# Self-attention values kept at 64 features a head, q and k projected for the second-next batch, and the layer norms' ends moved to the next score stage

## The chip, the cores and the metric

One core of a Trainium2 chip runs the whole kernel in one launch. The metric is the device time of one execution in microseconds (us). The core has four compute engines that the text calls TensorE (PE in the rows; PEld is its weight load), VectorE (DVE), ScalarE (ACT) and GpSimd (POOL), and SyncE (SP), which here only issues the DMAs. Each runs its own list of instructions strictly in order; semaphores join them.

## What is computed

The input x has 16 batches of 256 tokens with 128 features, in float32. Each batch passes through one decoder layer:

```python
x = layernorm(x + attn(x))        # 16 heads of 64, two null keys and values, ALiBi bias, causal
x = layernorm(x + xattn(x, ctx))  # 16 heads of 8 features, 64 context tokens
x = layernorm(x + ffn(x))         # eight groups of two batches; 128 -> 512 -> 128, no activation between
# inside attn, for a normalised xn:
q, k = l2norm(xn @ w_q) * q_scale, l2norm(xn @ w_k) * k_scale
sim = q @ k.T * 8 - slope[h] * distance      # masked above the diagonal
out = concat_heads(softmax(sim) @ (xn @ w_v)) @ w_out
```

## The kernel before, in words

All 16 batches are unrolled; `schedule` (L344) calls each engine's own `iteration(i, w, g)` for i = 0 to 15. A batch has two tiles t of 128 tokens. The order of the work is written out by hand, once for each engine, and the engines meet only through semaphores: whatever stands in an engine's list waits for what stands ahead of it. `stages(i)` (L350) says which parts exist at the ends of the loop. Iteration i does these things:

- **Score stage.** TensorE multiplies q and k of batch i (`scores`, L552) into the PSUM banks S0, S1 and S2. VectorE adds the bias and finds the row minimum of the negated score (`mask_scores`, L998, 32 instructions a batch). ScalarE takes the exponentials with their row sums (`exponentials`, L1315, 32 a batch). VectorE works out the denominators (`denominators`, L1015), and GpSimd multiplies the probabilities by them in 4 chunks for tile 0 and 8 for tile 1 (`norm_probs`, L1513).
- **Value products.** For each of the 12 chunks TensorE transposes four blocks of probabilities into bank T0 or T1 (`turn_probs`, L578), VectorE or ScalarE copies them to SBUF (`copy_pT`), and TensorE weighs the values with them (`weigh_values`, L589). Before the change w_v and w_out are multiplied together at the start (`merged_values`, `split_m`), so a head's values have 128 features and all heads add up in one PSUM tile `psY[t]`; the projection `project_v` (L528) then has 8 chunks of 512 columns. Every projection chunk is three matmuls, since the operands are split into two parts (`split_product`, L439).
- **q and k of batch i + 1**: `xn_turn` and `split_xnT`, 8 chunks of `project_qk` through the banks J0 and J1, of which VectorE copies three and ScalarE five, `square_qk` (ScalarE), `sum_squares` and `norms` (VectorE), `norm_qk` (GpSimd), `turn_qk`, `copy_qT`, `copy_kT`. This whole chain lies inside one iteration.
- **Second attention of batch i - 1** (`cross_scores`, `cross_shift`, `cross_exponentials`, `cross_denominators`, `norm_cross`, `turn_cross_probs`, `weigh_cross_values`, `merge_cross_heads`), its layer norm (ln3) and its feed-forward (`x2_turn`, `feed_forward`, `add_h2`), and half a layer norm more (`ln4_end` comes one iteration later). The layer norm after the first attention (ln2) and the turn of its result (`x1_turn`, `cross_q`) stand at the end of iteration i.

A layer norm is `ln_begin` (statistics, L844), a seed of the inverse root by ScalarE (`ln_seed`, L1249) and `ln_end` (L863): three small VectorE instructions that depend on one another (L857, L859, L861) and two of 128 x 128 (L870). `norms` has the same three small ones. `take` (L433) makes TensorE wait until the last reader of a PSUM bank is done.

## Time and profile before

| what | us |
|---|---|
| median of 3 runs | 1009.04 (1008.38 to 1009.17) |
| the profiled execution | 1014.34 |
| its span, first to last instruction | 1012.2 |

| engine | busy us | share of the span |
|---|---|---|
| TensorE | 849.9 | 84% |
| VectorE | 802.7 | 79% |
| ScalarE | 660.7 | 65% |
| GpSimd | 425.7 | 42% |

The profile is of one execution. An engine's busy time is the time in which at least one of its instructions runs; matmuls overlap, so the length of a single matmul is a latency, and what it costs is the distance from its start to the start of the next. The chain that ended last is 45% TensorE, 25% VectorE and 18% ScalarE.

### The profile page before, as it was taken

How to read it: one execution, taken by the hardware profiler on the slowest of the kernel's cores; microseconds unless marked ns; L12 is line 12 of the kernel's file. 1: busy time of each engine (PE TensorE's matmuls, PEld its weight loads, DVE VectorE, ACT ScalarE, POOL GpSimd, SP SyncE). 2: the span in 40 equal slices, each digit the busy share in tenths (PEclk: the TensorE clock that was granted, in tenths of full speed). 3: DMA queues.
4: the chain of work that ended last, by engine and by line, in shares of the span. 5: the costliest groups of instructions: out<-in, count | busy, mean ns of one | idle time of the engine just before them, and what ended most of it. 6: DMA issues, size and time to landing. Idle time of an engine off the chain costs nothing.

```text
span 1012.2 us, 18717 instructions
## 1 busy us (share of the span) xinstructions
PE 849.9 (84%) x6181; PEld 663.4 (66%) x6181; DVE 802.7 (79%) x2564; ACT 660.7 (65%) x1938; POOL 425.7 (42%) x356
## 2 busy tenths in 40 slices
PE   6898888888888898888889889888888888888774
PEld 5667666765766676576767657666765766676552
DVE  6665779788888978898897888788787988888545
ACT  4475767757685766767676675767667576766532
POOL 0244162543616253361635346173534617253431
PEclk9799999999999999999999999999999999999795
DMA  6000000000100000000100001000100001000000
GB/s 189 6 1 6 6 27 7 6 12 6 28 12 6 6 13 26 6 6 12 27 6 7 11 6 28 11 6 7 27 11 7 6 12 27 1 6 6 6 1 10
DMA packets 26414, 15.56 MB, mean 15 GB/s; under 512 B 4304, under 2 KB 25552, under 8 KB 26320
## 3 DMA queue, kind: packets, MB, share of 16 engines
q1 hardware_dynamic: 26320, 14.38, 5.0%
q8 instruction: 50, 0.82, 0.3%
q14 instruction: 44, 0.36, 0.1%
HBM read 12.27 MB, written 2.10 MB: 14 GB/s over the span
## 4 chain that ended last, share of the span: by engine, by line
PE 45%; DVE 25%; ACT 18%; issue 6%; POOL 4%; DMA 2%; DVEq 0%; ACTq 0%; POOLq 0%
PE psY L600 12%; ACT pr L1319 9%; PE psS L566 6%; PE psT L586 5%; PE psS L636 4%; ACT sq L1291 3%; POOL pr L1519 3%; PE psJ L441 3%; PE psS L548 3%; PE psJ L443 2%; PE psJ L442 2%; DVE xp L1061 2%; DVE xmax L1059 2%; DVE ssq L957 2%; ACT xpT L1367 2%
## 5 line engine op out<-in xcount | busy, mean ns | idle before, releaser
L1519 POOL TENSOR_TENSOR pr<-pr,rden 128x512 f32<-128x512 f32 x192 | 192.9, 1040 | 379.2 <-ACT pr L1319 195.8
L600 PE MATMUL psY<-val,pT 128*128 128x128 f32 x1536 | 206.5, 281 | 31.3 <-ACT pT L1334 23.7
L1319 ACT ACTIVATE pr<-pr,nmin 128x256 f32<-128x256 f32 (+1 forms) x512 | 225.3, 443 | 10.8 <-DVE nmin L1004 10.2
L600 PEld LDWEIGHTS psY<-val,pT 128*128 128x128 f32 x1536 | 186.6, 193 | 41.8 <-issue 22.2
L1004 DVE CUSTOM_DVE_ANT_0 pr<-psS,alibi,nullmin 128x256 f32<-128x256 f32 (+1 forms) x512 | 183.7, 414 | 26.4 <-PE psS L566 24.4
L1510 POOL TENSOR_TENSOR qk<-qk,rn 128x1024 f32<-128x1024 f32 x64 | 121.1, 1913 | 88.8 <-DVE x L870 50.2
L586 PE MATMUL psT<-ident,pr 128*128 128x128 f32 x768 | 116.9, 279 | 20.2 <-POOL pr L1519 20.2
L566 PE MATMUL psS<-kT,qT 64*128 64x256 f32 (+1 forms) x1024 | 111.7, 346 | 19.3 <-DVE nmin L1004 12.9
L586 PEld LDWEIGHTS psT<-ident,pr 128*128 128x128 f32 x768 | 88.9, 143 | 39.9 <-POOL pr L1519 32.7
L566 PEld LDWEIGHTS psS<-kT,qT 64*128 64x128 f32 x1024 | 78.2, 189 | 48.5 <-DVE nmin L1004 19.4
L1319 ACT ACTIVATION_READ_ACCUMULATOR pr<-pr,nmin 128x1 f32 x512 | 96.6, 189 | 0.0
L1304 ACT ACTIVATE val<-psJ 128x512 f32<-128x512 f32 x112 | 66.5, 594 | 25.6 <-PE psJ L443 25.1
L1059 DVE TENSOR_REDUCE xmax<-psS 128x8 f32<-128x512 f32 x64 | 43.9, 686 | 49.1 <-PE psS L636 49.1
L1334 ACT ACTIVATE pT<-psT 128x512 f32<-128x512 f32 x112 | 65.4, 585 | 26.3 <-PE psT L586 26.1
L957 DVE TENSOR_REDUCE ssq<-sq 128x16 f32<-128x1024 f32 x64 | 76.3, 1211 | 7.3 <-ACT sq L1291 5.9
L1283 ACT ACTIVATE qk<-psJ 128x512 f32<-128x512 f32 x80 | 47.5, 594 | 51.5 <-PE psJ L443 50.0
L441 PE MATMUL psJ<-wqk_hi,xnT_hi 128*128 128x512 f32 x128 | 61.9, 484 | 19.8 <-DVE xnT_lo L951 19.2
L1526 POOL TENSOR_TENSOR xp<-xp,xrden 128x1024 f32<-128x1024 f32 x32 | 60.9, 1902 | 29.2 <-DVE xrden L1068 28.5
L1367 ACT ACTIVATE xpT<-psT 128x512 f32<-128x512 f32 x64 | 37.7, 592 | 53.8 <-PE psT L660 53.7
L1028 DVE COPY pT<-psT 128x512 f32<-128x512 f32 x80 | 54.2, 677 | 21.6 <-PE psT L586 21.6
L548 PE MATMUL psS<-ident,qk 128*128 128x128 f32 x512 | 68.6, 278 | 2.3 <-DVE qT L994 2.3
L441 PEld LDWEIGHTS psJ<-wqk_hi,xnT_hi 128*128 128x128 f32 x128 | 24.9, 195 | 65.1 <-issue 31.5
(138 smaller groups left out, 1663.5 us busy)
## 6 DMA issues: line engine op xcount, KB each, us to landing
...
```

What stands on the lines that cost most here:

```text
L441: pe.matmul(dst, hi, whi, start=True, stop=False)
L548: mm = pe.transpose(psS[isk][:, P * j:P * (j + 1)], qk[t][:, col:col + P], ident[:])
L566: mm = pe.matmul(psS[score_bank(t, c)][:, keys * j:keys * (j + 1)], qT[r, h // 2, P * t:P * (t + 1)], kT[r, h // 2, 0:keys], start=True, s ...
L586: mm = pe.transpose(psT[c % 2][:, P * j:P * (j + 1)], pr[t][:, h, P * kt:P * (kt + 1)], ident[:])
L600: mm = pe.matmul(psY[t], pT[c % 4][:, P * j:P * (j + 1)], val[:, kt, P * h:P * (h + 1)], start=(blk == 0), stop=False)
L957: steps.mark(dve.tensor_reduce(ssq[:, t, H * half:H * (half + 1)], sq[:, HD * half:HD * (half + 1)].rearrange("p (h d) -> p h d", d=DH), A ...
L1004: dve.tensor_tensor_reduce(pr[t][:, h, :], psS[score_bank(t, c)][:, keys * j:keys * (j + 1)], alibi[:, h, SEQ - keys:SEQ], 1.0, nullmin[:, ...
L1304: act.activation(val[:, c // 4, 512 * (c % 4):512 * (c % 4) + 512], psJ[c % 2][:], ACT.Copy).then_inc(v_copied_act, 1)
L1319: act.activation(pr[t][:, h, :], pr[t][:, h, :], ACT.Exp, bias=nmin[:, t, h:h + 1], scale=-1.0, accum_out=dparts[:, t, h, 0:1]).then_inc(e ...
L1334: act.activation(pT[c % 4][:], psT[c % 2][:], ACT.Copy).then_inc(pT_copied_act, 1)
L1510: pool.tensor_tensor(v, v, rn[:, t, H * k:H * (k + 1)].unsqueeze(2).broadcast_to([P, H, DH]), ALU.mult).then_inc(qk_normed, 1)
L1519: pool.tensor_tensor(pr[t][:, hs, :], pr[t][:, hs, :], rden[:, t, hs].unsqueeze(2).broadcast_to([P, heads, P * (t + 1)]), ALU.mult).then_i ...
```

## The change

Values: w_v is split and used as it is, w_out stays in SBUF, `project_v` has 4 chunks instead of 8, and the product is turned around: the values (128 keys x 64 features) are the stationary operand, the transposed probabilities move, and the result of an even head lands in partitions 0 to 63, of an odd head in 64 to 127. Eight heads (a group) fill one bank, ScalarE copies it (`copy_aoT`, four a batch), and `join_heads` multiplies it by w_out, four matmuls a group. VectorE's copies of q, k and values all go to ScalarE.

Order: q and k are projected for batch i + 2 (two buffers for `qk`, `xnT`, `val`), the value projection of batch i + 1, the ends of ln3, of the feed-forward and of ln4 of batch i - 2, and `x1_turn` and `cross_q` of batch i - 1 stand in the score stage of iteration i, and `norm_qk` of batch i + 1 stands at GpSimd's head and between its two `norm_probs`. The input load of batch i + 3 takes the place of that of i + 2 at the head of SP's list. Iteration 0 does the q and k chain of batch 1 as well. Several buffers are shared (x1T, xoT and x2T; xpT and pT; x2b and r1), with waits for it. The diff, cut to its core:

```diff
 MASKED = 1e30
 
 QK_CHUNKS = 8
-V_CHUNKS = 8
-
-QK_DVE, QK_ACT = (0, 1, 3), (2, 4, 5, 6, 7)
-V_DVE, V_ACT = (2,), (0, 1, 3, 4, 5, 6, 7)
+V_CHUNKS = 4
+
+QK_DVE, QK_ACT = (), (0, 1, 2, 3, 4, 5, 6, 7)
 PT_DVE, PT_ACT = (0, 2, 6, 8, 10), (1, 3, 4, 5, 7, 9, 11)
...
 
 
...
             def project_v(n, c):
-                t, j = c // 4, c % 4
-                if isinstance(n, int) and n == 0 and c < 4:
-                    pe.wait_ge(m_split, 2 * (c // 2) + 2)
-                if c in V_ACT:
-                    take(f'J{c % 2}', v_copied_act, chunks_to(V_ACT, n, c))
-                else:
-                    take(f'J{c % 2}', v_copied_dve, chunks_to(V_DVE, n, c))
+                t, j = c // 2, c % 2
+                if isinstance(n, int) and n == 0 and c < 2:
+                    pe.wait_ge(wv_split, c + 1)
+                take(f'J{c % 2}', v_copied, V_CHUNKS * n + c + 1)
                 tok, col = slice(P * t, P * (t + 1)), slice(512 * j, 512 * (j + 1))
-                split_product(psJ[c % 2][:], xnT_hi[:, tok], xnT_lo[:, tok],
-                              m_hi[:, col], m_lo[:, col]).then_inc(v_ready, 1)
+                split_product(psJ[c % 2][:], xnT_hi[n % 2][:, tok], xnT_lo[n % 2][:, tok],
+                              wv_hi[:, col], wv_lo[:, col]).then_inc(v_ready, 1)
...
                 heads, keys = (4, P) if t == 0 else (2, SEQ)
-                if t == 0 and pair == 0:
-
-                    pe.wait_ge(kT_copied, 2 * NT * b + 1)
+                half = pair if t == 0 else pair // 2
+                pe.wait_ge(qT_copied, 2 * NT * b + 2 * t + half + 1)
+                pe.wait_ge(kT_copied, 2 * NT * b + 2 * t + half + 1)
...
             def turn_probs(b, c):
                 t, first = (0, 0) if c < TILE_PC[0] else (1, TILE_PC[0])
                 pe.wait_ge(probs_normed, PC * b + c + 1)
-                if c >= 2:
-                    evacuated(b, c - 2)
+                if c in PT_DVE:
+                    take(f'T{c % 2}', pT_copied_dve, chunks_to(PT_DVE, b, c))
+                else:
+                    take(f'T{c % 2}', pT_copied_act, chunks_to(PT_ACT, b, c))
...
+            def group_bank(t, g):
+
+                return ('S2', psS[2]) if t == 1 and g == 0 else ('Y', psY_bank)
+
             def weigh_values(b, c):
+
                 t, first = (0, 0) if c < TILE_PC[0] else (1, TILE_PC[0])
+                group = TILE_PC[t] // 2
+                g, within = divmod(c - first, group)
+                name, bank = group_bank(t, g)
                 if c == 0:
-                    pe.wait_ge(v_copied_dve, len(V_DVE) * (b + 1))
-                    pe.wait_ge(v_copied_act, len(V_ACT) * (b + 1))
-                if c == TILE_PC[0]:
-                    pe.wait_ge(y_added, NT * b + 1)
+                    pe.wait_ge(v_copied, V_CHUNKS * (b + 1))
+                if within == 0:
+                    take(name, aoT_copied, AC * b + 2 * t + g + 1)
                 evacuated(b, c)
-                for j in range(4):
+                blocks = [0, 1, 2, 3] if t == 0 else [0, 2, 1, 3]
+                for j in blocks:
                     blk = 4 * (c - first) + j
                     h, kt = blk // (t + 1), blk % (t + 1)
-                    mm = pe.matmul(psY[t], pT[c % 4][:, P * j:P * (j + 1)], val[:, kt, P * h:P * (h + 1)],
-                                   start=(blk == 0), stop=False)
+                    pair, r = h // 2 - 4 * g, slice(DH * (h % 2), DH * (h % 2) + DH)
+                    mm = pe.matmul(bank[r, P * pair:P * (pair + 1)], val[b % 2][:, kt, DH * h:DH * (h + 1)],
+                                   pT[c % 4][:, P * j:P * (j + 1)], start=(kt == 0), stop=(kt == t))
                 mm.then_inc(pv_done, 1)
+
+            def join_heads(b, t, g):
+
+                pe.wait_ge(aoT_copied, AC * b + 2 * t + g + 1)
+                if g == 0:
+                    take('Y' if t == 0 else 'S2', y_added, NT * b + t + 1)
+                for k in range(4):
+                    pe.matmul(psY[t], aoT[g][:, P * k:P * (k + 1)], wo[:, 4 * g + k, :],
+                              start=(g == 0 and k == 0), stop=False)
 
...
@@ -677,23 +683,23 @@
             def merge_cross_heads(b):
                 pe.wait_ge(xoT_copied, b + 1)
                 for t in range(NT):
-                    mm = pe.matmul(psS[2][:, P * t:P * (t + 1)], xoT[:, P * t:P * (t + 1)], xwo[:],
+                    mm = pe.matmul(psY_bank[:, P * t:P * (t + 1)], xoT[:, P * t:P * (t + 1)], xwo[:],
                                    start=True, stop=True)
                 mm.then_inc(y2_ready, 1)
 
             def x2_turn(b):
...
@@ -923,14 +945,13 @@
                         steps.mark(last)
                 last.then_inc(wn_split, 1)
 
-            def split_m(c):
-                dve.wait_ge(m_ready, c + 1)
-                hi, lo = (m[:].rearrange("p (c r d) -> p c r d", r=2, d=P)[:, 4 * (c // 2):4 * (c // 2) + 4, c % 2, :]
-                          for m in (m_hi, m_lo))
-                ps = psS[c % 2][:].rearrange("p (c d) -> p c d", d=P)
-                steps.mark(dve.tensor_copy(hi, ps))
+            def split_wv(c):
+                dve.wait_ge(vo_loaded, 16 * 2)
+                col = slice(512 * c, 512 * (c + 1))
+                steps.mark(dve.tensor_copy(wv_hi[:, col], wv_raw[:, col]))
                 steps.wait(dve)
-                dve.tensor_tensor(lo, ps, hi.bitcast(F32), ALU.subtract).then_inc(m_split, 1)
...
@@ -975,18 +997,14 @@
                 steps.wait(dve)
                 steps.mark(dve.tensor_tensor(nullneg[:], nullmul[:], nullbias[:], ALU.add))
                 steps.wait(dve)
-                steps.mark(dve.tensor_reduce(nullmin[:], nullneg[:].rearrange("p t (h n) -> p t h n", n=NULLS),
-                                             AX.X, ALU.min))
-                steps.wait(dve)
+                dve.tensor_reduce(nullmin[:], nullneg[:].rearrange("p t (h n) -> p t h n", n=NULLS),
+                                  AX.X, ALU.min).then_inc(nulls_scored, 1)
+                dve.wait_ge(nulls_scored, n + 1)
...
+                act.activation(val[n % 2][:, c // 2, 512 * (c % 2):512 * (c % 2) + 512], psJ[c % 2][:],
+                               ACT.Copy).then_inc(v_copied, 1)
+
+            def copy_aoT(b, t, g):
+                act.wait_ge(pv_done, PC * b + (TILE_PC[0] if t else 0) + (TILE_PC[t] // 2) * (g + 1))
+                bank = psS[2] if t == 1 and g == 0 else psY_bank
+                act.activation(aoT[g][:], bank[:], ACT.Copy).then_inc(aoT_copied, 1)
 
             def copy_kT(n, k):
                 t, half = k // 2, k % 2
...
             def copy_xqT(b):
                 act.wait_ge(xqT_ready, b + 1)
-                act.activation(xqT[:], psJ[1][:, 0:SEQ], ACT.Identity, bias=xb[:, 0:1]).then_inc(xqT_copied, 1)
+                act.activation(xqT[:], psT[1][:, 0:SEQ], ACT.Identity, bias=xb[:, 0:1]).then_inc(xqT_copied, 1)
...
             copy_qk(0, 4)
             copy_qk(0, 5)
```

The order of a full, odd iteration after the change, read off the diff, one list for each engine:

```
PE:
scores(i,0,0); x1_turn(i-1); project_v(i+1,0); scores(i,0,1); cross_q(i-1); project_v(i+1,1); scores(i,1,0);
x2_turn(i-2); project_v(i+1,2); scores(i,1,1); feed_forward(i-2); project_v(i+1,3); turn_probs(i,0); scores(i,1,2);
turn_probs(i,1); turn_nulls(i,0); weigh_values(i,0); turn_probs(i,2); scores(i,1,3); weigh_values(i,1);
turn_probs(i,3); weigh_values(i,2); weigh_values(i,3); cross_scores(i-1,0); xn_turn(i+2); join_heads(i,0,0);
join_heads(i,0,1); weigh_nulls(i,0); turn_probs(i,4); turn_probs(i,5); turn_nulls(i,1); cross_scores(i-1,1);
project_qk(i+2,0); weigh_values(i,4); turn_probs(i,6); weigh_values(i,5); turn_probs(i,7); merge_ffn(g);
turn_qk(i+1,0); turn_qk(i+1,1); weigh_values(i,6); turn_probs(i,8); project_qk(i+2,1); weigh_values(i,7);
turn_probs(i,9); turn_qk(i+1,2); turn_qk(i+1,3); turn_ffn(g); weigh_values(i,8); turn_probs(i,10);
project_qk(i+2,2); weigh_values(i,9); turn_probs(i,11); join_heads(i,1,0); project_qk(i+2,3); weigh_values(i,10);
project_qk(i+2,4); weigh_values(i,11); turn_cross_probs(i-1,0); turn_cross_probs(i-1,1); project_qk(i+2,5);
join_heads(i,1,1); weigh_nulls(i,1); turn_qk(i+1,4); turn_qk(i+1,5); weigh_cross_values(i-1,0);
turn_cross_probs(i-1,2); turn_cross_probs(i-1,3); turn_qk(i+1,6); turn_qk(i+1,7); project_qk(i+2,6);
weigh_cross_values(i-1,1); project_qk(i+2,7); merge_cross_heads(i-1); project_nulls(i+2)
DVE:
add_y2(i-2); sum_squares(i+1,1,0); mask_scores(i,0,(0,1)); sum_squares(i+1,1,1); floor_squares(1); ln3_begin(i-2);
mask_scores(i,0,(2,3)); null_shift(i,0); ln3_end(i-2); norms(i+1,1); mask_scores(i,1,(0)); mask_scores(i,1,(1));
denominators(i,0); mask_scores(i,1,(2)); mask_scores(i,1,(3)); add_h2(i-2); copy_pT(i,0); mask_scores(i,1,(4));
mask_scores(i,1,(5)); copy_pT(i,2); mask_scores(i,1,(6)); mask_scores(i,1,(7)); null_shift(i,1); denominators(i,1);
ln4_end(i-2); cross_shift(i-1,0); cross_shift(i-1,1); split_xnT(i+2); cross_shift(i-1,2); add_y(i,0);
cross_shift(i-1,3); ln1_begin(i+3); copy_pT(i,6); cross_denominators(i-1,0); copy_qT(i+1,0); copy_pT(i,8);
cross_denominators(i-1,1); ln1_end(i+3); copy_qT(i+1,1); copy_pT(i,10); null_scores(i+1); sum_squares(i+2,0,0);
sum_squares(i+2,0,1); floor_squares(0); add_y(i,1); ln2_begin(i); copy_qT(i+1,2); ln2_end(i); norms(i+2,0);
copy_qT(i+1,3)
ACT:
copy_v(i+1,0); exponentials(i,0,(0)); copy_x1T(i-1); exponentials(i,0,(1)); copy_v(i+1,1); qk_seed(i+1,1);
ln_seed(ln3,i-1); copy_xqT(i-1); exponentials(i,0,(2,3)); null_exponentials(i,0); exponentials(i,1,(0));
copy_x2T(i-2); exponentials(i,1,(1,2)); copy_v(i+1,2); exponentials(i,1,(3)); copy_v(i+1,3); copy_pnT(i,0);
copy_pT(i,1); exponentials(i,1,(4,5)); copy_aoT(i,0,0); ln_seed(ln4,i-1); copy_pT(i,3); exponentials(i,1,(6,7));
null_exponentials(i,1); copy_aoT(i,0,1); cross_exponentials(i-1,0); copy_pT(i,4); copy_pT(i,5); copy_pnT(i,1);
cross_exponentials(i-1,1); copy_qk(i+2,0); ln_seed(ln1,i+4); copy_pT(i,7); copy_w12raw(g); copy_kT(i+1,0);
copy_qk(i+2,1); copy_kT(i+1,1); copy_aoT(i,1,0); copy_pT(i,9); copy_w12(g); square_qk(i+2,0,0); copy_qk(i+2,2);
copy_pT(i,11); copy_qk(i+2,3); copy_qk(i+2,4); copy_aoT(i,1,1); square_qk(i+2,0,1); copy_xpT(i-1,0);
copy_xpT(i-1,1); ln_seed(ln2,i+1); copy_qk(i+2,5); copy_kT(i+1,2); qk_seed(i+2,0); copy_xpT(i-1,2); copy_xpT(i-1,3);
copy_kT(i+1,3); copy_qk(i+2,6); copy_xoT(i-1); copy_qk(i+2,7); square_qk(i+2,1,0); square_qk(i+2,1,1);
copy_nullraw(i+2)
POOL:
x1_plus_bias(i-1); norm_qk(i+1,0); x2_plus_bias(i-2); norm_probs(i,0); norm_qk(i+1,1); spread_values(i);
norm_probs(i,1); spread_keys(i); norm_cross(i-1)
```

## Rows read from the trace of the kernel before

**Rows 1.** Busy time of each engine in four stretches: start, batch 0, two later batches.
```profile
core 0: us, PE busy (x) PEld busy (x) DVE busy (x) ACT busy (x) POOL busy (x), PEclk, DMA share, GB/s
0.00:46.86 46.86, 36.16 (x183) 28.26 (x183) 31.30 (x90) 22.34 (x53) 7.72 (x8) 0.85 0.34 103
46.86:105.41 58.55, 51.16 (x356) 40.09 (x356) 34.40 (x116) 37.22 (x108) 22.05 (x19) 0.91 0.02 6
519.78:578.21 58.43, 49.99 (x373) 39.09 (x373) 50.11 (x159) 40.30 (x120) 26.62 (x22) 1.00 0.03 8
578.21:637.37 59.16, 51.32 (x382) 40.31 (x383) 49.02 (x159) 40.80 (x123) 26.60 (x22) 1.00 0.06 17
```
**Rows 2.** Costliest groups of instructions: value products, copies, exponentials, squares.
```profile
L600 PE MATMUL psY<-val,pT 128*128 128x128 f32 x1536 | 206.5, 281 | 31.3 <-ACT pT L1334 23.7 <-DVE pT L1028 7.5
...
L985 DVE COPY qk<-psJ 128x512 f32<-128x512 f32 x48 | 33.0, 688 | 1.8 <-PE psJ L443 1.8
...
L1319 ACT ACTIVATE pr<-pr,nmin 128x256 f32<-128x256 f32 (+1 forms) x512 | 225.3, 443 | 10.8 <-DVE nmin L1004 10.2
...
L1304 ACT ACTIVATE val<-psJ 128x512 f32<-128x512 f32 x112 | 66.5, 594 | 25.6 <-PE psJ L443 25.1
...
L1291 ACT ACTIVATE sq<-qk 128x1024 f32<-128x1024 f32 x64 | 65.6, 1050 | 1.3 <-DVE ssq L963 1.3
```
**Rows 3.** Timeline of TensorE: start, length, instructions.
```profile
73.43 3.76 PE L492 MATMUL psJ<-xw,xp 128*64 128x128 f32 x64 [0.17 <-ACT kTx L1272]
...
77.12 1.09 PE L586 MATMUL psT<-ident,pr 128*128 128x128 f32 x8
...
611.94 1.06 PE L600 MATMUL psY<-val,pT 128*128 128x128 f32 x8
...
612.83 0.60 PE L586 MATMUL psT<-ident,pr 128*128 128x128 f32 x4
...
631.85 0.48 PE L441 MATMUL psJ<-m_hi,xnT_hi 128*128 128x512 f32 x1
...
632.63 0.38 PE L688 MATMUL psJ<-ident,x 128*128 128x128 f32 x2
```
**Rows 4.** Timeline of VectorE in one batch: four of its waits.
```profile
580.52 0.48 DVE L949 TENSOR_SCALAR xnT_hi<-psJ,gam 128x256 fp32r<-128x256 f32 x1 [1.38 <-PE psJ L501]
...
598.40 0.69 DVE L1059 TENSOR_REDUCE xmax<-psS 128x8 f32<-128x512 f32 x1 [1.86 <-PE psS L636]
...
603.04 0.69 DVE L1059 TENSOR_REDUCE xmax<-psS 128x8 f32<-128x512 f32 x1 [1.28 <-PE psS L636]
...
614.98 0.52 DVE L857 TENSOR_TENSOR newt<-seedq 128x32 f32<-128x32 f32 x1 [1.51 <-ACT seedq L1247]
```
**Rows 5.** Three lines of VectorE by themselves: durations min/median/max in ns.
```profile
L853 DVE TENSOR_SCALAR ln_ve<-ln_mv x64: 168/170/1229, 3.7 to 1008.0; 128x2 f32<-128x2 f32 x64
...
L963 DVE TENSOR_SCALAR ssq<-ssq x32: 181/328/1133, 22.6 to 912.9; 128x32 f32<-128x32 f32 x32
...
L976 DVE TENSOR_TENSOR nullneg<-nullmul,nullbias x16: 224/1808/1895, 39.1 to 917.1; 128x64 f32<-128x64 f32 x16
```
**Rows 6.** Timeline of VectorE: three instructions of unusual length.
```profile
624.02 1.23 DVE L853 TENSOR_SCALAR ln_ve<-ln_mv 128x2 f32<-128x2 f32 x1
...
625.40 1.81 DVE L976 TENSOR_TENSOR nullneg<-nullmul,nullbias 128x64 f32<-128x64 f32 x1
...
993.58 1.75 DVE L861 SCALAR_TENSOR_TENSOR ln_rs<-ln_nw,ln_sd 128x2 f32<-128x2 f32 x1
```
**Rows 7.** Timeline of GpSimd: what it ran then, and its longest stretch.
```profile
600.36 8.02 POOL L1519 TENSOR_TENSOR pr<-pr,rden 128x512 f32<-128x512 f32 x8 [9.17 <-DVE rden L1019]
...
623.32 3.81 POOL L1510 TENSOR_TENSOR qk<-qk,rn 128x1024 f32<-128x1024 f32 x2 [3.53 <-DVE x L870]
...
993.40 1.91 POOL L1526 TENSOR_TENSOR xp<-xp,xrden 128x1024 f32<-128x1024 f32 x1 [2.19 <-DVE xrden L1068]
```
**Rows 8.** Waits of TensorE for a copy that it had just caused.
```profile
PE psS L672 <- ACT xpT L1367: 26.5, 32, 1.2
```

571 lines of the change are left out of this document (312 added, 259 removed).

## The prediction

> **What bounds the kernel now.** I read the page first: TensorE is busy for 84% of the span and VectorE for 79%, and no engine is full, so order and waits count beside work. The table by stretches comes next [rows 1]. The batches in the middle repeat with two periods, 58.43 and 59.16 us, 58.8 on the mean, and the granted clock of TensorE is 1.00 in them, its 2.4 GHz level. Of 59.16 us TensorE is busy for 51.3, VectorE for 49.0, ScalarE for 40.8 and GpSimd for 26.6. VectorE thus stands still for 10.1 us of each period, TensorE for 7.8. The groups of instructions [rows 2] give the prices, the timeline of TensorE [rows 3] the real distance between its instructions, and the timeline of VectorE [rows 4] where it stands still: 1.38 us for the turned input, 1.86 and 1.28 us for the second attention's scores, 1.51 us for a seed by ScalarE, with the rest in smaller pieces. Each of these is a step that VectorE asks for right after it was caused. That is the kind of wait which working further ahead removes.
>
> **Value projection.** A chunk of three matmuls takes 0.78 us from its start to the next instruction [rows 3]. Eight chunks become four: TensorE -3.1 us a period.
>
> **Value product.** Eight instructions of a chunk take 0.89 us before (611.94 to 612.83), 0.11 each [rows 3]. After the change each has a stationary tile of 64 columns, alternately in one half of the array and the other. The trace has just this form once: 64 instructions of form 128*64 with 128 moving columns in 3.76 us, one started each 0.055 us [rows 3], so the halves work at the same time. The way back to the full array is dearer: the last of these 64 started at about 76.92, the transpose behind it at 77.12, 0.15 us more than the beat. A chunk then costs 8 x 0.055 + 0.15 + a little for the way in, about 0.62 us, and 12 chunks save 12 x 0.27 = 3.2 us. The way in has no row; its bounds are 0 and the 0.15 of the way out, and I take 0.03, as nothing stands behind such an entry in the rows. At the other end 12 x 0.12 = 1.4 us a period come back.
>
> The Trainium skill (TensorEngine Tiling (Array Packing), Key Properties) says that a change of the tiling mode drains TensorE, and this change makes 24 such a batch. By it the way in would cost as the way out, and 14 periods would be 14 x 1.4 = 20 us longer in all.
>
> **Joining the heads** adds four groups of four matmuls, two instructions each (as 1536 instructions are 16 batches of 12 chunks of four [rows 2]): 32 x 0.11 = +3.5 us. TensorE comes to 51.3 - 3.1 - 3.2 + 3.5 = 48.5 us a period.
>
> **Copies.** VectorE loses three copies of q and k and one of values, 0.69 us long, of which the next instruction's start covers a little, so 0.6: -2.4 us, 49.0 to 46.6. ScalarE gets three of q and k (0.59, by the same reason 0.5), loses three of values, and gets the four new group copies: +2.0 us, 40.8 to 42.8 [rows 1, 2]. GpSimd has the same work. So no engine has more than 48.5 us to do, against a period of 58.8.
>
> **What is moved.** The score stage now holds ln3's and the feed-forward's ends, the second tile's sums of squares and the value projection. ScalarE's exponentials, 225.3 / 16 = 14.1 us a batch [rows 2], are its core; with four value copies, three small copies, three seeds and three of the value product's copies I add 6.5 us, so 20.6, and VectorE's list there comes to 20 us. The two run side by side, one chunk behind the other: about 21 us. Now that stretch is some 21 us too, but with less in it. The rest of the period is then 34 us instead of 38. Its list on VectorE has 26 us, on TensorE 30.
>
> **Waits that go, by VectorE's list.** Of 10.1 us still now, the 1.38 (input turned earlier, behind the heads' joining), the 1.86 (filled by the denominators and ln4's end) and the 1.51 (seed asked for an iteration ahead) go: -4.7. The 1.28 stays, since the second tile's cross scores still need the banks that VectorE has just read. New ones: `sum_squares(i+2,0,1)` stands right behind the first half, while ScalarE has a 1.05 us square, a group copy and two more copies ahead of it (1.5 us) [rows 2], and at the head of the score stage `sum_squares(i+1,1,0)` waits until the last q and k chunk was projected, copied and squared, about 0.8 + 0.6 + 1.0 behind VectorE (1.5 us). Behind these stands all of `mask_scores`, and behind that ScalarE. Left: 10.1 - 4.7 + 3.0 = 8.4 us.
>
> **VectorE against GpSimd.** Some VectorE instructions take far longer than their own work: L853 has 170 ns as its median and 1229 at most, L976 224 at least and 1808 as its median [rows 5]. On the timeline they end just when a GpSimd instruction ends: the 1.23 us one at 625.25 and the 1.81 us one at 627.21, with GpSimd's pair of 1.9 us running from 623.32 to 627.13; the 1.75 us one at 995.33, with GpSimd's from 993.40 to 995.31 [rows 6, 7]. They are instructions from SBUF to SBUF; the reads of PSUM show no such length. In the present period they cost 1.06 + 1.58 + about 0.6 = 3.2 us. The change moves `null_scores` and the first floor of the squares to where GpSimd has nothing left to do: -3.2. But it puts `ln4_end` right behind `denominators(i,1)`, which sets GpSimd's eight 1.0 us instructions going [rows 7], and `ln1_end` beside the second attention's two of 1.9 us. Each has three dependent small instructions and then two of 128 x 128. The cheapest is that none is held (0), the dearest that every dependent step waits for one GpSimd instruction: 4 x 1.0 + 2 x 1.9 = 7.8 us. I take 2.5 for ln4, 1.5 for ln1 and 0.5 for the small ones in the score stage, 4.5 in all, as in the one pair of rows the instruction right behind a held one slipped through and the next was held again.
>
> The Trainium skill (SBUF — State Buffer, section "SBUF: two separate sides") calls this an exclusive lock: whichever engine starts first holds the shared pair for the whole instruction. The rows agree to 0.1 us; it speaks against the new place of `ln4_end`.
>
> **The period after**, by VectorE: 46.6 - 3.2 + 4.5 + 8.4 = 56.3 if each wait were full; some of the held time takes the place of waits (ln4's end is held while VectorE would wait for cross scores), for which I take off 1.3: **55.0 us**, 3.8 less than 58.8.
>
> **The ends.** Before batch 0 [rows 1] the four splits of the merged matrix (a cast and a subtraction of the copies' shape, some 1.3 us each on VectorE) become two: -3 us (between 0 and -5). Iteration 0 gets a second batch's q and k chain, partly in the open: TensorE 8 x 0.78 = 6.2, ScalarE 8 x 0.5 + 4 x 1.0 = 8: +6 (0 to +10). Iteration 14 is free of its q and k chain: -8 (-4 to -9). Iteration 15 and the tail: two value chunks less, `x1_turn` and `cross_q` now behind the loop: 0. Sum -5. SP's list gains nothing: one input load is asked for an iteration earlier, and no load is waited for in the rows.
>
> **Sum.** 14 x -3.8 = -53, and -5: -58 us on the profiled execution's 1014.3 us (its span 1012.2 and 2.1 around it), so 956. The runs' median, 1009.04, lies 5.3 under it: 951 us.
>
> **Rivals.** (A) *VectorE is hardly held*, and the three new waits stay small: 46.6 - 3.2 + 1 + 8 = 52.4, 14 x -6.4 - 5 = -95, 914 us. For it: the timeline shows instructions that slipped in between. Against: four of them depend on one another. (B) *Held at every step*: 3 us more than I took, nearly all ahead of `cross_shift`, so ahead of ScalarE's `cross_exponentials`, behind which stand the copies of the probabilities and TensorE's value products. Period 58, 14 x -0.8 - 5: 993 us. (C) *Slower: the score stage turns serial.* `cross_q`, `feed_forward` and the group joins stand ahead of scores and transposes in TensorE's list, and each waits for a small copy that stands in ScalarE's list behind four exponentials (14.1 / 32 = 0.44 each, 1.8 us). A wait of TensorE for a copy it has just caused is 26.5 / 32 = 0.83 us now [rows 8]; seven such at 0.8, and not hidden, are 5.6 us. It decides once more than 4.2 us of them reach the path, a period over 59.2; at 60 the time is 14 x 1.2 - 5 = +12, 1021 us. Against it: the scores are needed some 3 to 6 us after they can start. (D) *The halves don't work in turn* when each chunk is between transposes: 0.11 instead of 0.055, and both ways at 0.15, 12 x (0.89 + 0.30 - 0.62) = +6.8 us on TensorE, 55.3 busy of a period of 61: 1035 us. Against it: the 64 instructions in rows 3.
>
> **How the numbers follow.** The forecast has 0.56, A 0.19, B 0.13, C 0.06, D 0.02, and 0.04 is for a time that stays within 0.2% (2 us), about what a measurement of this kernel can tell from no change. The forecast's own spread is 1.5 us of period either way, 930 to 972. The range takes in A and most of B: 912 to 992. Faster 0.88, same 0.04, slower 0.08.
>
> **What would show it.** In the profile after: `weigh_values` in groups of eight started every 0.055 us and a chunk of about 0.6 us to the next transpose; TensorE about 48 us busy in a period, VectorE about 48; L857, L859, L861 or L870 of ln4's end with lengths near 1 us; a wait of VectorE for the squares at the head of the score stage; `cross_q` and `feed_forward` with no wait behind them on VectorE. The forecast is wrong if the period is outside 53.5 to 56.5, if TensorE is busy over 51 us of it, or if the ends bring more than 10 us either way.

## The result and the profile after

The changed kernel takes 1049.73 us (median of 4 runs, 1046.64 to 1049.85) against 1009.11 us for the kernel before on the same chip, a ratio of 1.0395, 95% interval 1.0375 to 1.0416. It is 4% slower; the forecast was 951 us, 6% faster. The profiled execution spans 1047.6 us against 1012.2.

The page's first part and three of its groups of instructions come first. The columns of a group are: line, engine, operation, tiles and shapes, count | busy us, mean ns of one | idle time ahead of it and what ended that.

```profile
PE 856.9 (82%) x6469; PEld 609.2 (58%) x6469; DVE 772.6 (74%) x2496; ACT 671.2 (64%) x2002; POOL 424.7 (41%) x356
...
L1377 ACT ACTIVATE xp<-xp 128x1024 f32<-128x1024 f32 x32 | 33.8, 1057 | 152.2 <-DVE xp L1082 152.2
...
L978 DVE TENSOR_REDUCE ssq<-sq 128x16 f32<-128x1024 f32 x64 | 77.9, 1218 | 62.6 <-ACT sq L1313 62.2
...
L643 PE MATMUL psS<-kexp,xqT 64*128 64x512 f32 x128 | 49.9, 863 | 51.1 <-DVE xp L1082 50.5
```

Two of the same groups in the kernel before:

```profile
L636 PE MATMUL psS<-kexp,xqT 64*128 64x512 f32 x128 | 38.0, 668 | 20.7 <-DVE xp L1061 20.6
...
L1347 ACT ACTIVATE xp<-xp 128x1024 f32<-128x1024 f32 x32 | 33.8, 1057 | 14.3 <-DVE xp L1061 14.1
```

The engines have little more to do: VectorE falls from 802.7 to 772.6 us, TensorE has 7 us more and ScalarE 10.5, where the span grows by 35. What grows is waiting. ScalarE's second-attention exponentials (14.3 us of waits before, 152.2 now) and TensorE's second-attention scores (20.7 and 51.1) both wait for the same VectorE instruction, L1082, the last of `cross_shift`. So something on VectorE ahead of L1082 is late.

The stretches of the same profile, in the columns of [rows 1]: iteration 0, iteration 1, and two from the middle, each from its first scores to the next ones.

```profile
43.33:117.17 73.84, 58.91 (x421) 43.12 (x421) 39.72 (x138) 45.99 (x129) 23.36 (x20) 0.90 0.03 8
117.17:172.78 55.61, 48.52 (x397) 34.80 (x397) 40.80 (x133) 40.86 (x121) 23.73 (x20) 1.00 0.06 16
...
537.81:597.06 59.25, 50.71 (x394) 35.66 (x393) 48.25 (x154) 40.59 (x123) 26.52 (x22) 0.94 0.03 8
597.06:658.85 61.79, 53.04 (x404) 37.49 (x403) 47.73 (x154) 41.47 (x126) 26.52 (x22) 0.92 0.06 16
```

Iterations 2 to 13 take 60.96 us on the mean (172.78 to 904.34), against 58.78 before: +26 us of the span's +35. Iteration 0 takes 11.1 us more. Iteration 1 takes 55.61 us (59.08 before). It has no `ln4_end`, which begins at i = 2, and TensorE's granted clock is 1.00 in it; in iterations 2 to 13 it is 0.91 to 0.97, where the kernel before has 1.00 [rows 1]. That is a hint and no proof, as iteration 1 lacks the rest of batch i - 2's work too (VectorE is busy for 40.8 us in it, against some 48). These two differences, the place of `ln4_end` and the clock, are what the experiments take apart.

VectorE's timeline behind the last denominators (start, length, instruction), in the stretch 597.06:658.85:

```profile
621.32 0.20 DVE L1035 TENSOR_REDUCE den<-dparts 128x16 f32<-128x48 f32 x1 [2.09 <-ACT dparts L1352]
...
621.96 0.15 DVE L879 TENSOR_TENSOR ln_small<-ln_small 128x2 f32<-128x2 f32 x1
622.14 0.89 DVE L881 SCALAR_TENSOR_TENSOR ln_small<-ln_small 128x2 f32<-128x2 f32 x1
623.07 0.96 DVE L883 SCALAR_TENSOR_TENSOR ln_small<-ln_small 128x2 f32<-128x2 f32 x1
624.07 2.03 DVE L892 TENSOR_SCALAR x<-r,ln_mv,ln_small 128x128 f32<-128x128 f32 x2
626.01 0.68 DVE L1080 TENSOR_REDUCE xmax<-psS 128x8 f32<-128x512 f32 x1
```

GpSimd and TensorE in the same microseconds:

```profile
621.96 8.04 POOL L1580 TENSOR_TENSOR pr<-pr,rden 128x512 f32<-128x512 f32 x8 [3.45 <-DVE rden L1037]
```

```profile
628.88 2.08 PE L643 MATMUL psS<-kexp,xqT 64*128 64x512 f32 x4 [3.40 <-DVE xp L1082]
```

The eight GpSimd instructions of 1.0 us begin at 621.96, and from then on each VectorE instruction of `ln4_end` but the first ends about when one of GpSimd's does: at 623.03, 624.03, and 626.1 for the two of 128x128. It takes 4.1 us. Behind it stands `cross_shift`, and behind that TensorE, for 3.40 us.

What follows is in the granted clock, the third column from the right. Here the score stage and the standstill of TensorE are in windows of 2.06 us:

```profile
601.18:603.24 2.06, 1.15 (x5) 0.86 (x5) 1.89 (x8) 2.06 (x12) 0.43 (x1) 1.00 0.01 4
603.24:605.30 2.06, 1.05 (x10) 0.76 (x8) 2.06 (x15) 2.00 (x9) 0.00 (x0) 1.00 0.01 4
605.30:607.36 2.06, 0.87 (x7) 0.54 (x4) 1.88 (x10) 2.06 (x12) 0.51 (x1) 0.93 0.00 0
607.36:609.42 2.06, 1.81 (x6) 0.97 (x7) 2.03 (x9) 2.06 (x12) 0.21 (x1) 0.50 0.00 0
...
625.90:627.96 2.06, 0.00 (x0) 0.00 (x0) 2.02 (x4) 0.00 (x0) 2.06 (x3) 0.90 0.21 64
627.96:630.02 2.06, 1.14 (x4) 0.53 (x4) 1.62 (x4) 1.25 (x2) 2.04 (x3) 0.50 0.00 0
630.02:632.08 2.06, 2.06 (x7) 0.83 (x3) 1.08 (x2) 0.92 (x3) 1.03 (x1) 0.50 0.00 0
632.08:634.14 2.06, 2.06 (x13) 1.34 (x12) 2.02 (x6) 0.21 (x1) 0.01 (x1) 0.50 0.00 0
634.14:636.20 2.06, 2.06 (x20) 1.54 (x19) 1.92 (x6) 2.03 (x5) 0.00 (x0) 0.94 0.00 0
```

TensorE falls to its 1.2 GHz level twice in this period: in the score stage, where it is busy about half of the time, and after the standstill. The second fall is the worse one: 6.5 us at half speed (627.5 to 634.1), in 5.2 of which TensorE is full, so about 2.6 us of its work are lost.

### The profile page after: what moved, and what is told of

Its sections match the earlier page's. It is cut to its first block and busy times, and to the rows that moved or that the text cites. A ratio compares the mean times of both kernels' runs of the same rounds, so it can differ in the third digit from the quotient of the medians.

```text
span 1047.6 us, 19543 instructions
## 1 busy us (share of the span) xinstructions
PE 856.9 (82%) x6469; PEld 609.2 (58%) x6469; DVE 772.6 (74%) x2496; ACT 671.2 (64%) x2002; POOL 424.7 (41%) x356
## 5 line engine op out<-in xcount | busy, mean ns | idle before, releaser
L553 PE MATMUL psS<-kT,qT 64*128 64x256 f32 (+1 forms) x1024 | 121.6, 368 | 33.5 <-DVE nmin L1022 33.3
L1377 ACT ACTIVATE xp<-xp 128x1024 f32<-128x1024 f32 x32 | 33.8, 1057 | 152.2 <-DVE xp L1082 152.2
L575 PE MATMUL psT<-ident,pr 128*128 128x128 f32 x768 | 126.7, 293 | 1.5 <-POOL pr L1580 1.5
L553 PEld LDWEIGHTS psS<-kT,qT 64*128 64x128 f32 x1024 | 85.3, 201 | 63.3 <-issue 60.1
L1613 POOL TENSOR_TENSOR x1b<-x,bo 128x256 f32<-128x256 f32 x16 | 11.7, 734 | 244.6 <-DVE r L1094 222.7
L1305 ACT ACTIVATE qk<-psJ 128x512 f32<-128x512 f32 x128 | 76.0, 596 | 48.7 <-PE psJ L443 48.5
L598 PE MATMUL psY<-pT,val 128*64 128x128 f32 x1024 | 83.6, 285 | 11.6 <-DVE pT L1048 6.6
L643 PE MATMUL psS<-kexp,xqT 64*128 64x512 f32 x128 | 49.9, 863 | 51.1 <-DVE xp L1082 50.5
L598 PEld LDWEIGHTS psY<-pT,val 128*64 128x64 f32 x1024 | 53.7, 136 | 46.0 <-issue 27.9
L1313 ACT ACTIVATE sq<-qk 128x1024 f32<-128x1024 f32 x64 | 65.7, 1054 | 0.0
```

The lines of the kernel that those rows point to most:

```text
L553: mm = pe.matmul(psS[score_bank(t, c)][:, keys * j:keys * (j + 1)], qT[r, h // 2, P * t:P * (t + 1)], kT[r, h // 2, 0:keys], start=True, s ...
L575: mm = pe.transpose(psT[c % 2][:, P * j:P * (j + 1)], pr[t][:, h, P * kt:P * (kt + 1)], ident[:])
L598: mm = pe.matmul(bank[r, P * pair:P * (pair + 1)], val[b % 2][:, kt, DH * h:DH * (h + 1)], pT[c % 4][:, P * j:P * (j + 1)], start=(kt == 0 ...
L1305: act.activation(qk[n % 2][t][:, 512 * j:512 * (j + 1)], psJ[c % 2][:], ACT.Copy).then_inc(qk_copied_act, 1)
L1313: act.activation(sq[:, col], qk[n % 2][t][:, col], ACT.Square).then_inc(qk_squared, 1)
```

## The experiments

The theory that they test has two parts. **Hold**: `ln4_end`, placed behind the denominators, is held by GpSimd's instructions, and the second attention's chain stands behind it. **Clock**: wherever TensorE stands still or half still, it then runs at its lower level, which costs as much again. The rivals: the values' new form or the new waits for it are the cost, or the two engines slow each other in another way. The period is always the mean of iterations 2 to 13, taken from the windows of each profile; "before" is 58.78 and "changed" 60.96 us.

**1. `ln4_end` ahead of the denominators.** The changed kernel with two lines swapped:

```diff
                 null_shift(i, 1)
-                denominators(i, 1)
                 if e:
                     ln4_end(i - 2)
+                denominators(i, 1)
```

> The changed kernel (1049.7 us) with one step moved: ln4_end(i-2) stands ahead of denominators(i,1) on VectorE, so before GpSimd's eight instructions start, in the 2.09 us in which VectorE waits there anyway. Theory H+C (ln4_end is held by GpSimd for 2.9 us, TensorE stands still behind it for 3.4 us and then runs some 7 us at its 1.2 GHz level): both go, the period falls from 61.0 to about 56.5, 14 of them, so about 987 us. Theory H alone (the low clock has another origin and stays): 2.9 x 14 = 40 us less, about 1010. Theory R (TensorE's later list sets the period and the hold is slack): within 5 us of 1050.

Measured: 985.82 us (984.72 to 986.15), ratio to before 0.9758 (0.9739 to 0.9778), period 56.54. VectorE's timeline of the same place:

```profile
587.79 0.15 DVE L879 TENSOR_TENSOR ln_small<-ln_small 128x2 f32<-128x2 f32 x1
587.97 0.16 DVE L881 SCALAR_TENSOR_TENSOR ln_small<-ln_small 128x2 f32<-128x2 f32 x1
588.17 0.16 DVE L883 SCALAR_TENSOR_TENSOR ln_small<-ln_small 128x2 f32<-128x2 f32 x1
588.37 0.60 DVE L892 TENSOR_SCALAR x<-r,ln_mv,ln_small 128x128 f32<-128x128 f32 x2
589.95 0.20 DVE L1035 TENSOR_REDUCE den<-dparts 128x16 f32<-128x48 f32 x1 [0.98 <-ACT dparts L1352]
```

The same five instructions take 1.2 us instead of 4.1, and they fill half of a wait that VectorE has anyway, the 2.09 us for ScalarE's null exponentials (the wait is still 0.98 us). Nothing is taken out of the kernel, and 64 us go: a change that was 4% slower than before is now 2.4% faster. Of the 64 us, 12 x 4.42 = 53 lie in the middle periods and most of the rest behind them.

**2. GpSimd's instructions cut in halves.** This asks for the mechanism of the hold. Nothing moves; only the length of GpSimd's instructions changes.

```diff
-                    hs = slice(heads * c, heads * (c + 1))
-                    pool.tensor_tensor(pr[t][:, hs, :], pr[t][:, hs, :],
-                                       rden[:, t, hs].unsqueeze(2).broadcast_to([P, heads, P * (t + 1)]),
-                                       ALU.mult).then_inc(probs_normed, 1)
+                    for part in range(t + 1):
+                        n = heads // (t + 1)
+                        hs = slice(heads * c + n * part, heads * c + n * (part + 1))
+                        last = pool.tensor_tensor(pr[t][:, hs, :], pr[t][:, hs, :],
+                                                  rden[:, t, hs].unsqueeze(2).broadcast_to([P, n, P * (t + 1)]),
+                                                  ALU.mult)
+                    last.then_inc(probs_normed, 1)
```

> The changed kernel with each of GpSimd's eight probability multiplications of tile 1 (128x512, 1.0 us) cut into two of 128x256; the same work, nothing else moved. GpSimd's stretch grows by the fixed part of eight more instructions, by the rows of its 512 and 1024 forms (1.04 and 1.91 us) about 0.17 us each, 1.4 us. Theory H (a VectorE instruction of ln4's end that starts beside a GpSimd instruction ends with it, so the hold is as long as one GpSimd instruction): the lengths of 0.89, 0.96 and 1.0 us become about 0.5 to 0.6, ln4's end takes 2.5 to 2.8 us instead of 4.1, the standstill of TensorE 2 us instead of 3.4, the period 59 to 60 and the time 1018 to 1037 us. Rival (the two engines slow each other in proportion, whatever the length of an instruction): ln4's end still takes 4 us, the time is 1045 to 1065 us.

Measured: 1011.07 us (1008.66 to 1016.72), ratio 1.0034 (1.0015 to 1.0054), period 58.09. VectorE and, in the second fence, GpSimd:

```profile
604.18 0.15 DVE L879 TENSOR_TENSOR ln_small<-ln_small 128x2 f32<-128x2 f32 x1
604.37 0.46 DVE L881 SCALAR_TENSOR_TENSOR ln_small<-ln_small 128x2 f32<-128x2 f32 x1
604.86 0.54 DVE L883 SCALAR_TENSOR_TENSOR ln_small<-ln_small 128x2 f32<-128x2 f32 x1
605.44 1.17 DVE L892 TENSOR_SCALAR x<-r,ln_mv,ln_small 128x128 f32<-128x128 f32 x2
```

```profile
604.18 9.20 POOL L1582 TENSOR_TENSOR pr<-pr,rden 128x256 f32<-128x256 f32 x16 [3.45 <-DVE rden L1037]
```

The held lengths follow GpSimd's instruction down: 0.89, 0.96 and about 1.0 us become 0.46, 0.54 and about 0.6, and `ln4_end` takes 2.4 us instead of 4.1. GpSimd itself works 1.2 us longer, and yet the kernel is 39 us faster. The time lies below the 1018 to 1037 us expected: I had put in the 1.7 us of hold and little else, but the period falls by 2.87 us. The other 1.2 us fit TensorE's clock behind the shorter standstill, though no run separates them:

```profile
607.00:609.00 2.00, 0.70 (x7) 0.42 (x5) 1.93 (x4) 0.00 (x0) 2.00 (x5) 1.00 0.22 66
609.00:611.00 2.00, 1.60 (x4) 0.51 (x4) 1.13 (x3) 1.71 (x3) 2.00 (x4) 0.62 0.00 0
611.00:613.00 2.00, 2.00 (x7) 0.88 (x5) 1.55 (x4) 0.46 (x2) 2.00 (x5) 0.53 0.00 0
```

It stands still for 1.70 us instead of 3.40, and is at half speed for some 3.5 us, not for 6.5. The rival, that the engines slow each other in proportion whatever the length of an instruction, falls with the lengths.

The Trainium skill (SBUF — State Buffer, section "SBUF: two separate sides") has the shared port pair taken for a whole instruction by the engine that starts first; that a shorter instruction shortens the hold agrees with it, 0.46 us against 0.89.

**3. Useless matmuls where TensorE stands**, in both places and then in one. A filler is a matmul of up to 512 columns whose result nobody reads. The diff leaves out the conditions at the loop's ends and the waits for the last reader of each filler's bank.

```diff
+            def fill(bank, first, count):
+                for _ in range(count):
+                    pe.matmul(psJ[bank][:, first:512], ident[:], wo[:].rearrange("p c d -> p (c d)")[:, first:512],
+                              start=True, stop=True)
...
+                fill(0, 0, 1)                 # first run only
                 scores(i, 1, 0)
+                fill(0, 0, 1)                 # first run only
...
                 turn_probs(i, 5)
+                fill(1, P, 5)                 # both runs
                 turn_nulls(i, 1)
```

> The changed kernel with useless matmuls where TensorE stands still: five of 384 columns behind turn_probs(i,5), one of 512 before scores(i,1,0) and one behind it (0.64 and 0.85 us each at 2.4 GHz, 4.9 us a batch; their results are never read). Nothing else moves, ln4_end stays held. Theory C (each standstill drops TensorE to 1.2 GHz for the next 4 to 7 us and this costs some 4 us a period): granted clock near 1.00 in the middle periods, period 57 to 58.5, about 1000 us, although work was added. Theory H alone or R: the clock does not matter to the path, and 4.9 us more work leaves 1050 or makes it longer, up to 1090.

> The changed kernel (1049.73 us, mean period 60.96) with the five useless matmuls in the 3.4 us standstill ahead of the second tile's cross scores alone, none in the score stage (with both: 1028.06 us). Theory: the fall of the clock behind the standstill (7 us at half speed, with TensorE full) is the dear one, the other lies beside VectorE and ScalarE: 1028 to 1036 us. Rival: the score stage's fall costs at least half: 1038 us or more.

With both: 1028.06 us (1027.75 to 1032.82), ratio 1.0189 (1.016 to 1.0219), period 59.43, clock 1.00 in every middle period. I had expected about 1000 us and a period of 57 to 58.5, as I put the clock at some 4 us a period: the direction came, 22 us less with more work, but not half of the size. In the standstill alone: 1032.65 us (1029.51 to 1035.03), ratio 1.0216 (1.0172 to 1.026), period 59.56, clock 0.94 to 1.00. Iteration 1 of the second run, where TensorE doesn't stand and so nothing hides the filler, takes 58.82 us instead of 55.61: the five matmuls are 3.2 us of work. In the later periods these 3.2 us more work make the period 1.4 us *shorter*. The filler in the score stage, 1.7 us of work, brings another 0.13 us a period: a fall of the clock there lies beside VectorE and ScalarE, which carry that stage. So the dear fall is the one behind the standstill, and at least 1.4 us a period of the changed kernel is clock.

**4. The same hold in the kernel before.** `ln4_end(i - 2)` is moved there from between the masks of tile 1 to behind `denominators(i, 1)`, and in a second run five fillers (4.3 us) are put where TensorE then stands.

```diff
-                    if k == 4 and e:
-                        ln4_end(i - 2)
...
                 denominators(i, 1)
+                if e:
+                    ln4_end(i - 2)
                 if c:
                     cross_shift(i - 1, 1)
```

> The kernel before (1009.1 us) with one step moved, the reverse of the first run: ln4_end(i-2) taken out of mask_scores and put behind denominators(i,1), where GpSimd has just started its eight instructions; the first cross_shift stays ahead of it. Theory H: ln4_end takes 4.1 us instead of 1.2 there and delays cross_shift(1) and cross_scores(1); part of it is paid back in the score stage: +2 to +3 us a period, about 1040. Theory C on top: TensorE stands still for over 3 us there and drops its clock, +3 more, up to 1080. If the hold is harmless: 1009 within 4 us.

> The kernel before with ln4's end behind the denominators (1085.05 us, period 64.25, TensorE still for 5.05 us ahead of the second tile's cross scores and then at 0.50 to 0.71 of its clock for 8.4 us) plus five useless matmuls of 512 columns, 4.3 us, where TensorE stands. It separates the held VectorE instructions from the clock. Theory K: the clock is 1.00 again, the held steps stay, the period is 60.5 to 61.5 (58.8, and 2 to 3 us that ln4's end is held), the time 1030 to 1048 us. Rival H (the hold alone costs the 5.5 us, and the clock's part is hidden by other engines): the period stays at 64 and the time at 1080 to 1090 us.

Without filler 1085.05 us (1083.94 to 1089.17), ratio 1.075 (1.0721 to 1.0779), period 64.28; with it 1070.68 us (1067.51 to 1072.56), ratio 1.0585 (1.0547 to 1.0622), period 62.77. In the windows of the first run TensorE isn't busy at all for 4 us and then has half a clock:

```profile
317.70:319.70 2.00, 0.00 (x0) 0.00 (x0) 1.93 (x3) 0.28 (x1) 2.00 (x3) 1.00 0.00 0
319.70:321.70 2.00, 0.00 (x0) 0.00 (x0) 1.97 (x4) 0.00 (x0) 2.00 (x3) 0.72 0.00 0
321.70:323.70 2.00, 1.30 (x4) 0.53 (x4) 0.55 (x1) 1.06 (x1) 2.00 (x3) 0.50 0.22 66
```

One instruction group of 1.2 us, moved by a few places, costs 5.5 us a period: 1.5 that the filler gives back (clock), and 4.0 that stay. The filler itself isn't in these 4.0 at that place, as TensorE still waits 0.75 us for `cross_shift` behind it. I had expected 2 to 3 for the latter (1030 to 1048 us), and missed by counting only the extra length. Here too `ln4_end` takes 4.1 us, and all of it now stands between the denominators and `cross_shift`, where its 1.2 us had stood among the masks. The price of a late group fits its whole held length, not only the growth.

**5. The values alone**, in the old order: 64 features a head, `join_heads`, 4 value chunks, and all that is needed for them; q and k, the norms' ends and the second attention stay where they were. The score stage thereby loses the value projection's chunks 6 and 7. A second run puts one filler in each of those two places.

```diff
                 scores(i, 0, 0)
-                project_v(i, 6)
+                fill(0, 0, 1)                 # second run only
                 scores(i, 0, 1)
-                project_v(i, 7)
+                fill(1, 0, 1)                 # second run only
```

> The kernel before with only the values' part of the change: 64 features a head, four projection chunks, the turned product, four group copies by ScalarE and join_heads; q and k still one batch ahead, norms and cross attention where they were, VectorE still copies three q and k chunks. TensorE has 2.4 to 2.8 us less a period, half of it on the path: about 990 us if the values' part is sound. If the values' part is what made the change slow (four new handovers to ScalarE, or a freed TensorE that loses its clock): 1020 to 1045 us.

> The kernel before with the values alone changed (1035.96 us, period about 60.5) plus one useless matmul of 512 columns in each of the two places of the score stage from which the value projection's chunks 6 and 7 had gone: 2 x 0.85 us of work more a batch. Theory K (what cost values-alone its time is TensorE's clock: it stood still at the head of the score stage and then ran at the lower level for some 6 us): the granted clock of the middle periods is back at 0.99 or 1.00, the period 57.5 to 59, the time 985 to 1010 us. Rival W (the new waits for group copies and shared banks are the cost, the clock follows from them): the period stays at 60 or grows by up to the 1.7 us of added work, 1030 to 1060 us.

The first: 1035.96 us (1033.01 to 1041.03), ratio 1.0247 (1.0217 to 1.0277), period 61.05, with these windows at the start of a score stage:

```profile
225.65:227.65 2.00, 1.09 (x16) 0.90 (x16) 1.76 (x11) 0.77 (x4) 0.00 (x0) 1.00 0.27 74
227.65:229.65 2.00, 1.45 (x16) 1.48 (x16) 1.49 (x12) 2.00 (x13) 0.00 (x0) 0.72 0.00 0
229.65:231.65 2.00, 0.98 (x6) 0.36 (x3) 0.94 (x3) 0.81 (x5) 0.00 (x0) 0.50 0.00 0
231.65:233.65 2.00, 1.83 (x5) 1.11 (x7) 2.00 (x16) 1.67 (x9) 0.00 (x0) 0.50 0.00 0
233.65:235.65 2.00, 2.00 (x9) 1.18 (x10) 0.92 (x5) 1.63 (x9) 0.00 (x0) 0.57 0.00 0
```

The second: 1018.21 us (1015.08 to 1022.93), ratio 1.0077 (1.0051 to 1.0104), period 59.70, clock 1.00 in all middle periods but the last (0.97). Taking 1.6 us of work out of the score stage cost full clock for 8 us of that period, and putting useless work in its place saves 18 us. The expectation of 985 to 1010 us is missed all the same: 0.9 us a period stay that aren't clock. VectorE's waits for the second attention's scores are 54.1 us in that run against 49.1 before, which fits the joins of tile 0, as they stand ahead of the second tile's scores in TensorE's list. And one wait is new, that of `add_y` for TensorE's last product of the attention, which `join_heads` now stands ahead of (us in all, times, the longest):

```profile
DVE r L1039 <- PE psS L617: 27.7, 16, 5.1
```

In the kernel before `add_y` waits for 4.1 us in all. So the trace has more new waits than the 12 x 0.92 = 11 us ask for. Which of them reach the path wasn't tried, nor whether the fillers, 1.7 us of work, are part of it, so this remainder stays open. Two things are seen, then: values alone lose the clock, and with useless work that keeps it they are still no gain in the old order.

**6. From the first experiment on**: fillers in the score stage; then `ln1_end` away from GpSimd's `norm_cross`; then, from the first of these, useful work in place of one of the two fillers of an odd iteration. The diff leaves out that ScalarE's `copy_w12raw` moves into the score stage with it.

```diff
 # second run: VectorE
-                if d:
-                    ln1_end(i + 3)
                 if a:
                     copy_qT(i + 1, 1)
                 copy_pT(i, 10)
                 if a:
                     null_scores(i + 1)
+                if d:
+                    ln1_end(i + 3)
 # third run: TensorE, ahead of scores(i, 1, 0)
+                if w:
+                    merge_ffn(g)
...
-                    if w and k == 5:
-                        merge_ffn(g)
```

> The changed kernel with ln4's end ahead of the denominators (985.82 us, mean period 56.5, granted clock 0.97 in most periods) plus two useless matmuls of 512 columns in the score stage, 1.7 us of TensorE a batch. Theory K: the clock is 1.00 in all middle periods and the 2 us in 4 us at the lower level go; as TensorE isn't the engine that the score stage waits for, that gives back 0.3 to 1 us a period: 972 to 982 us. Rival: the added work stands ahead of scores that VectorE waits for: +0.5 to +1.5 us a period, 993 to 1007 us.

> The best kernel so far (ln4's end ahead of the denominators, two fillers: 980.7 us, periods 55.3 and 57.1) with ln1's end behind null_scores, where GpSimd has nothing to run, so that its one held step (1.75 us instead of 0.16) goes. Theory: TensorE is busy without a gap in that stretch and VectorE isn't waited for, so the 1.6 us buy nothing: 978 to 983 us, VectorE's busy time a period down by 1.5. Rival: VectorE's list carries the second half of the period, and 13 x 1.6 us come back: 958 to 968 us.

> The 980.7 us kernel with the product of the feed-forward's two matrices, and its two small copies by ScalarE, in the score stage of the odd iterations, where it replaces the filler; in its old place TensorE waits 1.45 us for a copy and then takes 1.0 us for it. Odd periods are 57.1 us and even ones 55.3. Theory: TensorE carries the second half of the period, so 2.4 us go there, and the score stage, which ScalarE and VectorE carry, grows by the copies' 0.5 us: odd periods 55.2 to 55.8, time 968 to 973 us. Rival (the score stage grows as much as the rest shrinks, because ScalarE's exponentials stand behind the copies and the copies behind the product): odd periods 56.5 to 57.5, 977 to 985 us.

The fillers: 980.7 us (980.24 to 982.19), ratio 0.9701 (0.9673 to 0.9729), period 56.24, with a clock of 1.00 in all middle periods. With `ln1_end` moved as well: 981.34 us (979.37 to 984.65), ratio 0.9732 (0.9711 to 0.9753), period 56.26. The third, from the first of these: 969.1 us (967.83 to 969.55), ratio 0.9603 (0.9587 to 0.9619), period 55.32. One even period of each of the first two, and an even and an odd one of the third:

```profile
395.33:450.67 55.34, 49.78 (x397) 34.98 (x397) 45.86 (x154) 40.79 (x123) 26.47 (x22) 1.00 0.03 8
```

```profile
396.44:451.76 55.32, 49.81 (x397) 34.97 (x396) 44.35 (x154) 40.75 (x123) 26.48 (x22) 1.00 0.03 8
```

```profile
391.67:447.00 55.33, 49.81 (x398) 34.97 (x397) 45.84 (x154) 40.78 (x123) 26.48 (x22) 1.00 0.03 8
447.00:502.57 55.57, 50.09 (x406) 35.94 (x405) 45.85 (x154) 41.17 (x126) 26.48 (x22) 1.00 0.07 18
```

The second is the control: VectorE is busy 1.5 us less in a period, a hold like that of `ln4_end` is gone, and the period is the same to 0.02 us, since TensorE is busy without a gap in that stretch (429.96 to 453.61 in the profile of the first) and waits for nothing that stands behind it. This hold costs nothing, because nobody waits. The third moves 1.0 us of TensorE's work, with a 1.45 us wait for a copy ahead of it, out of the stretch that TensorE carries into the stage where it has room; the odd periods go from 57.1 to 55.6, 1.5 us of the 2.4. It is the fastest kernel of the study, 3.97% faster than before and 7.7% faster than the change as it stood.

## Why the prediction was wrong

The forecast was a period of 55.0 us; measured are 60.96. All three of its signs of being wrong came: the period is outside 53.5 to 56.5, TensorE is busy for 51.8 us of it (over 51, as part of it runs at half speed), and the ends bring 12.8 us. VectorE is busy for 47.9 us of a period on the mean, which is the forecast's 46.6 - 3.2 + 4.5 to a tenth, so the miss lies in VectorE's idle time: 13.0 us against 8.4 - 1.3 = 7.1. Point by point:

- **Value product, value projection, joins: right, but for 0.7 us.** A chunk takes 0.58 us from its start to the next transpose (forecast 0.62), eight instructions on alternating halves. The sixteen of the two joins of tile 0 take 1.96 us to the next instruction (623.87), 0.12 each (0.11). TensorE is busy 49.2 us in a period of the first experiment at full clock (48.5). What is missing is the way in, for which I took 0.03 us: where nothing is waited for, a chunk's first instruction starts 0.20 us behind the transpose ahead of it in the trace, against 0.11 in the kernel before, so the way in is 0.09. With it a chunk costs 0.67, and 12 x 0.05 is most of the 0.7 us. The 0.15 that would have cost 20 us in all isn't seen either. Rival D is out.

```profile
617.10 0.66 PE L598 MATMUL psY<-pT,val 128*64 128x128 f32 x8
617.68 0.65 PE L575 MATMUL psT<-ident,pr 128*128 128x128 f32 x4
...
621.91 2.02 PE L608 MATMUL psY<-wo,aoT 128*128 128x128 f32 x16 [0.57 <-ACT aoT L1333]
```

- **How long VectorE is held: right.** I took 2.5 us for `ln4_end`, 1.5 for `ln1_end` and 0.5 for the small ones. Measured: 4.1 - 1.2 = 2.9; 1.75 - 0.16 = 1.6 on the timeline of `ln1_end`; and 0.72 - 0.19 = 0.5 for one step in the score stage. The sum is 5.0 against 4.5.
- **Where it is held: this step failed.** "Some of the held time takes the place of waits (ln4's end is held while VectorE would wait for cross scores), for which I take off 1.3." VectorE's wait for those scores is indeed gone at 626.01. But the scores of the other tile wait for `cross_shift`, so the time was handed on to TensorE (3.40 us) and ScalarE (7.0 us at most). The one wait that `ln4_end` could have filled stands ahead of the denominators, the 2.09 us for ScalarE's null exponentials, and I had not listed it: I took the old waits of VectorE and asked which go, and never asked what `denominators(i, 1)` would wait for when VectorE gets there earlier. The same list ends at 8.4 us still; in the period shown it is 61.79 - 47.73 = 14.1. Two of its waits the forecast doesn't have: 2.1 us for the null exponentials and 1.9 for the product that `add_y2` needs. The new waits for the squares were seen, and take 3.9 us (forecast 3.0).
- **TensorE's clock: not in the sum at all.** I read that the granted clock is 1.00 in the middle and let it stand. The trace of before says more: batch 0 has 0.91 and the start 0.85 [rows 1], and its last iteration, which I didn't look at in small windows, shows what a quiet TensorE brings:

```profile
932.31:936.31 4.00, 2.28 (x15) 1.46 (x16) 3.86 (x24) 3.52 (x18) 0.00 (x0) 1.00 0.00 0
936.31:940.31 4.00, 0.87 (x8) 0.47 (x6) 2.06 (x12) 4.00 (x21) 1.29 (x2) 0.83 0.00 0
940.31:944.31 4.00, 4.00 (x17) 2.56 (x17) 1.12 (x5) 1.97 (x9) 2.74 (x3) 0.50 0.00 0
```

  At least 1.4 us of the period (experiment 3) are clock. With the 2.9 us of hold that makes 4.3, close to the 4.42 that the first experiment gives back.
- **The sum again.** The first experiment takes 4.42 of the 5.96 us by which the period missed; score-stage fillers take 0.3, the feed-forward's product 0.9, and at 55.32 the period is the forecast's. So the forecast's period is reached with `ln4_end` and the feed-forward's product moved and the gaps filled, that is with another order than the change's: that 55 can be reached doesn't make the forecast right for the kernel that it was for.
- **Rivals.** B (held at every step, ahead of `cross_shift`) had the mechanism and its place: four of the five instructions of `ln4_end` end with one of GpSimd's. It had not the size, 7.5 us held in all against 5.0 measured, and it came to 993 us because it too had no clock and set the held time against waits. It deserved more than 0.13. C did not happen: from the first scores to the last mask is 22 us (forecast 21). A had no support.
- **The ends.** Forecast -5 us, measured +12.8 (start +0.7, iteration 0 +11.1, iteration 14 -3.8, iteration 15 and the tail +4.8). Iteration 0 is the largest miss: +11.1 instead of +6. With the values alone it takes 63.9 us, and with the new order 73.8, so the order makes it, and what that adds to iteration 0 is the second q and k chain. The trace shows parts of it in the open: VectorE waits 1.7, 2.3 and 4.7 us in it for ScalarE's squares and for the next turned input. The sum counts iteration 14 both among its 14 periods (-3.8) and here (-8), -11.8 in all; it gained 3.8, and has the hold and the clock as well; in the fastest kernel it takes 49.4 us, 9 less than before. The start can't be judged to 3 us: among the runs whose code there is that of before it varies from 40.3 to 42.9 us.
- **The order by itself** is a gain, but only by difference: 59.70 us (values alone) against 56.24 (all of the change, `ln4_end` early), each with two fillers of 512 columns in the score stage, 3.5 us a period. It wasn't run alone.
